# The start of a CIN tower kernel: shifted rows and pair tiles of the first chunk made by TensorE, stores and gathers moved

## The reference, cut to what matters

```python
e = jnp.stack([tbl_0[ids[:, 0]], ..., tbl_38[ids[:, 38]]], axis=1)      # (2048, 39, 16)
x0 = xk = e
for idx, (W, b) in enumerate([(w0, b0), (w1, b1), (w2, b2)]):           # W: (39, 39 or 64, 128)
    z = jnp.einsum('bhd,bkd,hks->bsd', x0, xk, W) + b[None, :, None]
    z = jax.nn.relu(z)
    if idx != 2:
        xk = z[:, :64, :]
        direct.append(z[:, 64:, :])
    else:
        direct.append(z)
z = jnp.sum(jnp.concatenate(direct, axis=1), axis=-1)                   # (2048, 256)
h = jnp.concatenate([z, dense_ctx], axis=1)
h = relu(h @ W_top1 + b_top1); h = relu(h @ W_top2 + b_top2); y = h @ W_top3
```

## Time and profile before

| | us |
|---|---|
| median of 3 runs | 2480.24 (2478.45 to 2482.26) |
| the profiled execution's own time | 2467.41 |
| its span, first to last instruction | 2465.7 |
| TensorE's mean granted clock in it, share of full | 0.997 |
| VectorE busy | 2229.2 (90%) |
| GpSimd busy | 1706.1 (69%) |
| ACT busy | 1484.1 (60%) |
| DMA, mean | 195 GB/s |

### The profile page before, as it was taken

How to read it: one execution, slowest core, us unless ns; L and a number is a source line. 1 busy time by engine, 2 the same in 40 slices (tenths; PEclk the granted TensorE clock), 3 DMA queues, 4 the chain that set the end, 5 groups by cost and what they waited for, 6 DMA issues and landing times.

```text
span 2465.7 us, 26690 instructions
## 1 busy us (share of the span) xinstructions
PE 2366.6 (96%) x7712; PEld 1456.0 (59%) x7712; DVE 2229.2 (90%) x1358; ACT 1484.1 (60%) x1766; POOL 1706.1 (69%) x1091
## 2 busy tenths in 40 slices
PE   0599999999999999999999999999999999999999
PEld 0266666666666666666666666666666666666653
DVE  0599999999999999999999999999999999999960
ACT  0366666666666666666666666666666666666642
POOL 6577777777777777777777777777777777754340
PEclk9999999999999999999999999999999999999999
DMA  2987878788787878878787887778778787877620
GB/s 70 249 229 183 211 211 211 188 216 224 189 204 213 217 183 213 221 199 196 214 223 188 207 217 211 187 210 224 195 199 220 214 185 209 218 205 186 201 63 0
DMA packets 380953, 481.10 MB, mean 195 GB/s; under 512 B 140683, under 2 KB 155771, under 8 KB 380853
## 3 DMA queue, kind: packets, MB, share of 16 engines
q1 hardware_dynamic: 260006, 275.13, 43.6%
q10 hardware_dynamic: 100480, 200.29, 28.8%
q0 software_dynamic: 20448, 5.45, 1.9%
HBM read 470.96 MB, written 9.84 MB: 195 GB/s over the span
## 4 chain that ended last, share of the span: by engine, by line
PE 95%; POOL 2%; DMA 2%; issue 1%; ACT 0%; DVE 0%; SPq 0%; ACTq 0%; POOLq 0%; DVEq 0%
PE z L735 46%; PE z L756 46%; POOL emb L394 1%; PE z L850 1%; PE xk L850 1%; DMA x_pairs<-x_transposed 1%; PE direct L850 1%; DMA x_diag<-x_transposed 0%; POOL lo_parts L244 0%; DVE prod L464 0%; DMA x_transposed<-emb 0%; ACT x_pairs L723 0%; DMA emb<-in_tbl,idx 0%; ACT hi_parts L586 0%; DMA idx<-in_ids 0%
## 5 line engine op out<-in xcount | busy, mean ns | idle before, releaser
L464 DVE TENSOR_TENSOR prod<-x_pairs,xk 128x2048 f32<-128x2048 f32 x640 | 1438.4, 2281 | 88.5 <-PE z L756 47.4
L735 PE MATMUL z<-prod,w_plain 128*128 128x512 f32 (+2 forms) x2688 | 1264.7, 595 | 91.6 <-DVE prod L464 91.6
L244 POOL TENSOR_TENSOR lo_parts<-prod,hi_parts 128x1024 fp32r<-128x1024 f32 x384 | 917.6, 2390 | 484.0 <-ACT hi_parts L586 458.3
L586 ACT CAST hi_parts<-prod 128x1024 fp32r<-128x1024 f32 x766 | 797.7, 1049 | 699.6 <-DVE prod L464 508.0
L756 PE MATMUL z<-hi_parts,w_lo 128*128 128x512 f32 (+1 forms) x1536 | 862.3, 561 | 1.1 <-DVE lo_parts L244 0.7
L394 POOL DMA_INDIRECT emb<-in_tbl,idx x624 | 698.9, 1120 | 192.5 <-issue 176.8
L735 PEld LDWEIGHTS z<-prod,w_plain 128*128 128x128 f32 (+2 forms) x2688 | 510.2, 190 | 491.1 <-issue 420.2
L756 PE MATMUL z<-hi_parts,w_hi 128*128 128x512 f32 (+1 forms) x1536 | 611.1, 398 | 0.0
L756 PE MATMUL z<-lo_parts,w_hi 128*128 128x512 f32 (+1 forms) x1536 | 606.5, 395 | 0.0
L756 PEld LDWEIGHTS z<-hi_parts,w_lo 128*128 128x128 f32 (+1 forms) x1536 | 289.9, 189 | 199.9 <-issue 151.0
L756 PEld LDWEIGHTS z<-lo_parts,w_hi 128*128 128x128 f32 (+1 forms) x1536 | 292.1, 190 | 193.0 <-issue 152.0
(11 more groups left out here) (64 smaller groups left out, 546.2 us busy)
## 6 DMA issues: line engine op xcount, KB each, us to landing
x_pairs<-x_transposed SPq DMA_DIRECT2D x64, 2432.0 KB, 16.5
x_pairs<-x_transposed ACTq DMA_DIRECT2D x64, 2432.0 KB, 18.9
x_diag<-x_transposed SPq DMA_DIRECT2D x128, 546.0 KB
x_diag<-x_transposed ACTq DMA_DIRECT2D x64, 546.0 KB
x_pairs<-x_transposed SPq DMA_DIRECT2D x64, 256.0 KB, 19.7
emb<-in_tbl,idx POOLq DMA_INDIRECT x624
x_diag<-x_transposed SPq DMA_DIRECT2D x128, 78.0 KB
x_transposed<-emb SPq DMA_DIRECT2D x16, 312.0 KB, 6.2
```

Source lines behind the costliest of these rows:

```text
L244: engine.tensor_tensor(lo_parts[0:rows, place:place + m, :], held[0:rows, at:at + m, :], hi, ALU.subtract).then_inc(done, 1)
L464: nc.vector.tensor_tensor(prod[0:rows, pos % RING, 0:n, :], a, xk.unsqueeze(1).broadcast_to([rows, n, N]), ALU.mult).then_inc(prod_ready, 1)
L586: nc.scalar.copy(hi_parts[0:rows, place:place + m, :], held[:, at:at + m, :]).then_inc(hi_ready, 1)
L735: return nc.tensor.matmul(z[n][:], w, held[0:rows, i, :], start=first, stop=last)
```

## The change

Chunk 0 of group 0 no longer gets its shifted rows, nor eight of its 20 pair tiles, from DRAM. When the first 39 gathers have landed, TensorE transposes the 32 examples' rows (16 transposes into `z[1]`), VectorE copies them to `rows0`, and TensorE multiplies selection matrices (made by VectorE from a banded identity that GpSimd makes first) with `rows0`: 7 shifted tiles, `xk0`, and pair tiles 12 to 19. ACT copies each from PSUM. SP stores the chunk's 32 rows first (`first_stored`), ACT the other 96 rows of the group (`xt_stored`); SP loads pair tiles 0 to 11 after `first_stored`.

Outside the first chunk: `load_chunk` loses its `store` argument. `store_group(bt)` now stands at the head of `load_chunk(bt, 0)`, so SP issues it at `c == 3` of its own loop, after the pair loads of `load_chunk(bt - 1, 3)`, with the wait for `xt_stored` right behind it. GpSimd gathers 14 fields ahead instead of 20; group 0 then takes 11, 11, 3 and 13 fields in its four chunks and starts group 2's at `c == 3` (`turn=3`); group 1 takes 13, 13, 10 and 10; from group 2 on the spread is as before, with the start at `c == 2`. VectorE's group 0 and GpSimd's groups 0 and 1 stand ahead of their loops.

```diff
-GATHERS_AHEAD = 20
+GATHERS_AHEAD = 14
+GATHERS_FIRST = [range(14, 25), range(25, 36), range(36, F), range(0, 13)]
+GATHERS_SECOND = [range(13, 26), range(26, F), range(0, 10), range(10, 20)]
 GATHERS_AT = [range(20, 30), range(30, F), range(0, 10), range(10, 20)]
+SPREAD_PAIRS = (16, 17, 18, 19, 12, 13, 14, 15)
+COPIED_PAIRS = 12
+SPREAD_EARLY = 3
...
+        spread_banks = [z[1], hi_copy[:, 0, :], hi_copy[:, 1, :]]
+        spread_to = ([x0_diag[0:R0, t, :] for t in range(T0)]
+                     + [x0_pairs[0][:, t, :] for t in SPREAD_PAIRS])
...
+            def first_chunk():
+
+                sp.wait_ge(gathered, 16 * F)
+                store_rows(sp, 0, 0, slice(0, CB), first_stored)
+                sp.wait_ge(first_stored, 16 * ST_DMAS)
+                sp.wait_ge(w_split, 3)
+                for half in range(2):
...
+                    sp.dma_start(x0_pairs[0][half * HALF:(half + 1) * HALF, 0:COPIED_PAIRS, :],
+                                 src.partition_broadcast(HALF)).then_inc(first_pairs_in, 16)
+                sp.wait_ge(xt_stored, 16 * ST_DMAS)
+
+            def load_chunk(bt, c):
...
                 if c == 0:
+                    store_group(bt)
                     sp.wait_ge(xt_stored, 16 * ST_DMAS * (bt + 1))
-                if not (isinstance(bt, int) and bt == c == 0):
-
-                    sp.wait_ge(summed2, sums)
+                sp.wait_ge(summed2, sums)
                 chunk = xt[:, bass.ds(first, N)]
                 for i in range(DIAG - 1):
                     diag_band(sp, chunk, i)
-                if store:
-                    store_group(bt + 1)
...
+                sp.wait_ge(prod_ready, slots)
                 pairs_half(sp, chunk, c, 0)
...
                     if c < CHUNKS - 1:
-                        load_chunk(bt, c + 1, c == 2 and not last)
+                        load_chunk(bt, c + 1)
                     elif not last:
                         load_chunk(bt + 1, 0)
...
-            def group(bt, fields_at):
+            def group(bt, fields_at, turn=2):
...
-                    if c == 2 and len(fields_at[c]):
+                    if c == turn and len(fields_at[c]):
                         start_group(bt + 2, False)
...
+            pool.wait_ge(first_stored, 16 * ST_DMAS)
+            pool.wait_ge(rows0_turned, 1)
             start_group(1, False)
             gather(range(0, GATHERS_AHEAD))
-            with pool.Fori(0, GROUPS - 2) as bt:
+            group(0, GATHERS_FIRST, 3)
+            group(1, GATHERS_SECOND)
+            with pool.Fori(2, GROUPS - 2) as bt:
                 group(bt, GATHERS_AT)
...
+            dve.wait_ge(rows0_turned, 1)
+            nc.vector.tensor_copy(rows0[:], z[1][0:F]).then_inc(rows0_ready, 1)
             dve.wait_ge(xk0_ready, 1)
-            late, split = products(0, x0_diag, xk0, 0, 0, [], 0, 0)
+            late, split = products(0, x0_diag, xk0, 0, 0, [], 0, 0, {0: QUAD, 1: T0})
...
+            act.wait_ge(gathered, 16 * F)
+            store_rows(nc.scalar, 0, 0, slice(CB, P), xt_stored)
+            take_spread(range(T0))
...
+            take_spread(range(T0, T0 + SPREAD_EARLY))
             hand_on(0, xk1, b0_sb, SL0)
             direct_0()
+            take_spread(range(T0 + SPREAD_EARLY, len(spread_to)))
+            act.wait_ge(spread_ready, len(spread_to))
+            act.wait_ge(xt_stored, 16 * ST_DMAS)
             load_last_band(0, 1)
...
+            for d in range(D):
+
+                ins = nc.tensor.transpose(z[1][0:F, d:N:D], emb[0:CB, d:F * D:D], ident[0:CB, 0:CB])
+            ins.then_inc(rows0_turned, 1)
+            pe.wait_ge(chosen_ready, T0 + 3)
+            pe.wait_ge(rows0_ready, 1)
+            spread_rows(range(QUAD))
+            nc.tensor.matmul(xk0[0:R0], by_diag[:, T0, :], rows0[:], start=True, stop=True
+                             ).then_inc(xk0_ready, 1)
+            spread_rows(range(QUAD, T0 + SPREAD_EARLY))
             pe.wait_ge(w0_summed, 2)
             pe.wait_ge(w_split, 3)
             pe.wait_ge(weights_in, 16 * WEIGHT_DMAS)
             layer0(0, 0, {V: 0, G: 0})
+            spread_rows(range(T0 + SPREAD_EARLY, len(spread_to)))
+            pe.wait_ge(spread_ready, len(spread_to))
```

More of the change, by code:

```diff
@@ L153, in build @@
         emb = sb("emb", [P, F * D])
+        ident = sb("ident", [F, F + WRAP])
+        rows0 = sb("rows0", [F, N])
+        by_diag = sb("by_diag", [F, T0 + 1, R0])
+        by_pair = sb("by_pair", [F, F + 1 - 2 * COPIED_PAIRS, HALF])
         w_plain = [sb(f"w{n}_plain", [P, len(PLAIN_TILES[n]), S]) for n in SPLITS]
@@ L245, in low_part, with chosen, store_rows @@
                                      hi, ALU.subtract).then_inc(done, 1)
+        spread_banks = [z[1], hi_copy[:, 0, :], hi_copy[:, 1, :]]
+        spread_to = ([x0_diag[0:R0, t, :] for t in range(T0)]
+                     + [x0_pairs[0][:, t, :] for t in SPREAD_PAIRS])
+        def chosen(first, *dims):
+            rows = ident[0:F, first:]
+            return bass.AP(tensor=rows.tensor, offset=rows.offset, ap=[rows.ap[0], *dims])
+        pair_columns = by_pair[:].rearrange("f g h -> f (g h)")
+        spread_by = ([by_diag[:, t, :] for t in range(T0)]
+                     + [pair_columns[:, (t - COPIED_PAIRS) * P:(t + 1 - COPIED_PAIRS) * P]
+                        for t in SPREAD_PAIRS])
+        def store_rows(engine, bt, first, parts, done):
+            cols = xt[:, bass.ds(first, P * D)].rearrange("f (b d) -> b f d", d=D)
+            rows = emb[:].rearrange("p (f d) -> p f d", d=D)
+            engine.dma_start(cols[parts, 0:F, :], rows[parts]).then_inc(done, 16)
+            engine.dma_start(cols[parts, F:F + WRAP, :], rows[parts, 0:WRAP, :]).then_inc(done, 16)
         def diag_band(engine, chunk, i):
@@ L288, in store_group @@
                 sp.wait_ge(gathered, 16 * F * (bt + 1))
[L289 to L294, removed]
+                store_rows(sp, bt, first, slice(0, P), xt_stored)
+            def first_chunk():
[4 more added lines that the diff above has]
+                for half in range(2):
+                    src = xt[half:half + 2 * COPIED_PAIRS, 0:N].rearrange(
+                        "(t two) n -> t two n", two=2)[:, 0, :]
+                    sp.dma_start(x0_pairs[0][half * HALF:(half + 1) * HALF, 0:COPIED_PAIRS, :],
+                                 src.partition_broadcast(HALF)).then_inc(first_pairs_in, 16)
+                sp.wait_ge(xt_stored, 16 * ST_DMAS)
+            def load_chunk(bt, c):
                 first = ahead(bt * (P * D) + c * N)
@@ L347, in load_top @@
                     sp.dma_start(dst, src).then_inc(top_weights_in, 16)
[L349 to L352, removed]
+            first_chunk()
             def group(bt, last):
@@ L379, in _ @@
         def _(pool):
+            nc.gpsimd.memset(ident[:], 0.0).then_inc(ident_zero, 1)
+            for i in range(2):
+                pool.wait_ge(ident_zero, i + 1)
+                nc.gpsimd.affine_select(out=ident[:], in_=ident[:], compare_op=ALU.not_equal,
+                                        fill=1.0, base=i * F, pattern=[[-1, F + WRAP]],
+                                        channel_multiplier=1
+                                        ).then_inc((ident_zero, ident_ready)[i], 1)
             def load_indices(bt):
@@ L488, in splits_of, with products @@
                 return here
-            def products(n, copies, xk, slot, pos, late, split, chunk):
+            def products(n, copies, xk, slot, pos, late, split, chunk, spread_in={}):
                 first_tile, rows, tiles = (FIRST_TILE, P, TX) if n else (L0_FIRST, R0, T0)
                 for k, first in enumerate(first_tile):
+                    if k in spread_in:
+                        dve.wait_ge(spread_ready, spread_in[k])
                     product(slot + k, pos + k, copies[0:rows, first:min(first + QUAD, tiles), :],
@@ L530, in group @@
                     copies = x0_pairs[c % 2]
-                    dve.wait_ge(x0_pairs_in[c % 2],
-                                16 * X0_PAIRS_DMAS * (bt * (CHUNKS // 2) + c // 2 + 1))
+                    first = isinstance(bt, int) and bt == c == 0
+                    if first:
+                        dve.wait_ge(first_pairs_in, 32)
+                        dve.sem_inc(x0_pairs_in[0], 16 * X0_PAIRS_DMAS)
+                    else:
+                        dve.wait_ge(x0_pairs_in[c % 2],
+                                    16 * X0_PAIRS_DMAS * (bt * (CHUNKS // 2) + c // 2 + 1))
                     dve.wait_ge(xk_ready[0], chunk + 1)
-                    late, split = products(1, copies, xk1, slot, pos, [], split, chunk)
+                    spread_in = {FIRST_TILE.index(t): T0 + QUAD * (i + 1)
+                                 for i, t in enumerate(SPREAD_PAIRS[::QUAD])} if first else {}
+                    late, split = products(1, copies, xk1, slot, pos, [], split, chunk, spread_in)
                     slot, pos = slot + SLX, pos + SLX
@@ L552, in group @@
```

(25 more changed lines are left out.)

27 lines of the change are left out of this document (21 added, 6 removed).

## The result

The changed kernel takes 2668.11 us (2667.10 to 2670.39), the kernel before 2480.68 in the same comparison: ratio 1.0758, 95% interval 1.0739 to 1.0776, slower by 187 us. The profiled execution of the changed kernel took 2667.10 us, its span is 2665.4, 199.7 longer than that of before.

A forecast was written before the change was run, and what follows sets the result against it. TensorE, busy 96% of the span, was taken as the bound. 173 (13 stands) + 0.7 + 2.5 + 6.2 - 17.8 = +164.6 us on the profiled 2467.41 gives 2632; carrying 12.8 to the median gives 2645 us, bounds 2610 to 2700.

The forecast's parts named there:

- The sign and the cause: Slower, chance 0.92: at `c == 2` GpSimd's gathers wait for the store behind the pair loads, 13 times, 173 us.
- The price of one stand: TensorE idle for late gathers at `c == 2`: 11.5 us standing plus 1.8 for the clock, 13.3 us [11.3 to 16.7].
- Why the store is late: SP's queue: the store, issued at about 741.4, is queued behind 2.7 MB of pair loads and lands at 765.5.
- ACT's wait: ACT waits for the store before the last band: 2.5 us in group 0, 0.7 in group 14, elsewhere inside the stall.
- Thirteen gathers: Chunks with thirteen gathers, in groups 0 and 1: 2.05 us each, three times, 6.2 us [4 to 12].
- The start: Ahead of TensorE's first full chunk: 17.8 us saved [12 to 21].
- five matmuls of 0.9 us: Start, after the copy to `rows0` at 58.0: four tiles and `xk0` done at 62.5, first product at 62.8.
- has worked since 54: Start: TensorE's six plain matmuls taken at full clock, so 11.0 us from the first product to `xk1`, at 73.8.
- The transposes: Start: 16 transposes on TensorE at the lower clock, 0.22 us each, 3.5 us [2.5 to 6.2], to 57.4.
- the first layer-1 product: Start: VectorE begins it at 74.5 [74 to 79.5] instead of 93.7, 19.2 us less.
- the stand's clock term: After each stand TensorE begins at the lower clock, four matmuls in 3.58 us instead of 1.72 to 1.8: 1.8 us.
- The signs named before: 13 TensorE dips, 13 GpSimd waits of some 15 us, store landing about 24, group period 156.5, half clock, first layer-1 product 74.5.

The follow-up runs named there:

- a_store_back: Changed kernel with the next group's store back between band loads and pair loads at `c == 2` from group 1 on; 2461.52 us, ratio 0.9969.
- b_store_moved: Kernel before with only the store moved to the head of `load_chunk(bt, 0)`, behind the pair loads; 2670.02 us, ratio 1.0813.
- c_store_ahead: As a_store_back, but the store issued after the wait for the chunk's first product, directly ahead of the pair loads; 2575.61 us, ratio 1.0433.
- i_one_queue: c_store_ahead with ACT's half of chunk 3's pair loads also issued by SP, behind the store; 2536.04 us, ratio 1.0274.
- d_turn3: Changed kernel with every group gathering 13, 13, 0 and 13 fields and starting the next but one group at `c == 3`; 2566.19 us.
- e_start_only: a_store_back with the store at its old place in every group, 20 gathers ahead and the old spread; 2449.43 us, ratio 0.9918.
- f_alloc_only: Kernel before with only the change's four new buffers allocated, unused; 2453.85 us, ratio 0.9938.
- j2_warm: e_start_only plus nine unused fp32 matmuls on TensorE ahead of the transposes, released behind GpSimd's 31st gather; 2453.64 us, ratio 0.9935.
- k2_padded: e_start_only with `rows0` and the selection matrices extended from 39 to 128 partitions, zeros in the added rows; 2440.58 us, ratio 0.9882.

## Why the prediction was right, step by step

- **The sign and the cause**: GpSimd's wait for the store at `c == 2` in 13 groups, named before. a_store_back and b_store_moved show it from both sides.
- **The price of one stand**: 13.3 forecast, 11.5 of standing and 1.8 for the clock. TensorE's 13 stands last 9.8 to 13.2 us, 12.1 on average; in the chunk shown the store landed 26.6 us after the pair loads' issue, where I had 25.6. The clock cost more than 1.8: behind a stand TensorE works at half for 3.0 to 6.1 us, 4.6 on average (5.7 in the chunk shown, 3.3 in the earlier trace rows), which costs 2.3. That makes 14.4. In b_store_moved, where nothing else differs, the whole is 200.7 us for 14 stands and group 14's 2.5: 14.2 each, of which 12.0 are standing and 2.1 the clock.
- **Why the store is late**: half right. I priced only what is ahead in SP's queue. c_store_ahead and i_one_queue split it: 18.0 us with ACT's pair loads beside it and nothing ahead, 7.1 with neither, 22.8 with both.
- **ACT's wait**: 2.5 forecast in group 0, 5.6 in the trace; 0.7 in group 14, where the trace has a chunk 2.6 us longer; in the other groups some 1 us by d_turn3, hidden in the stand.
- **Thirteen gathers**: 2.05 forecast, 1.9 to 3.1 measured in d_turn3; the three such chunks of the changed kernel cost 1.7, 2.9 and 3.2, 7.8 in all, where I had 6.2.
- **The start**: 17.8 forecast, 4.4 measured (e_start_only against f_alloc_only). This is the term that was mis-sized most. The step that failed is "five matmuls of 0.9 us": I read "x4" in the earlier trace rows as four matmuls, but an fp32 matmul stands as two in these rows. And I put TensorE at the full clock since it "has worked since 54"; it stayed at half through 19 us of 39-row matmuls. The stretches of this trace read 1.00 there, because its record of the clock begins with the first rise, at 80.0; the pace tells it: four rows ("x4") take 3.62 us, as they do in j2_warm at a recorded 0.50. What this cost is shown by k2_padded: 8.9 us less with the clock up from 62 us on. The changed kernel's rows:

```profile
56.85 2.02 PE L885 MATMUL z<-rows,by_diag 39*117 39x512 f32 x2 [0.87 <-DVE rows L581]
58.67 3.62 PE L885 MATMUL hi_copy<-rows,by_diag 39*117 39x512 f32 x4
...
65.74 2.29 DVE L513 TENSOR_TENSOR prod<-x_diag,xk 117x2048 f32<-117x2048 f32 x1 [9.04 <-PE xk L897]
...
84.87 4.48 DVE L513 TENSOR_TENSOR prod<-x_pairs,xk 128x2048 f32<-128x2048 f32 x2 [8.78 <-ACT xk L678]
...
92.15 1.04 ACT L657 CAST hi_parts<-prod 128x1024 fp32r<-128x1024 f32 x1 [2.16 <-issue]
```

  The first product is at 65.74, not 62.8, and `xk1`, not the pairs, comes last at 84.8. The transposes took 1.3 us where I had 3.5. Then ACT's last copies and DMA issues hold its first rounding back, 7.3 us behind the product instead of 3.25. So `xk1` was ready 11 us later than forecast, and the first layer-1 product, named as a sign at 74.5, started at 84.87. The misreading doesn't touch the stand's clock term, which compares equal rows.
- **What I had not**: the addresses, 15 us less; and 17 chunks of 36.1 instead of 35.56 us, with TensorE waiting 0.3 us for GpSimd in them, whose cause stays open.
- **The signs named before**: the 13 dips and GpSimd's 13 waits (15.2 to 17.4 us, some 15 forecast), the store's landing (22.8, about 24), the period of a group (157.9, 156.5) and the half clock in each stand are there. The first layer-1 product is not.
- **The total is nearer than its terms, and that is luck.** Between the two profiled executions the change costs 199.7 us; I had 164.6, 35 too few. Of these 35 the stands account for 14, the start for 13, group 0, group 14 and the thirteen gathers for 6 or 7; the addresses gave 15 back. What is left, some 16, are the 36.1 us chunks and losses near the stands that no run explains. In the comparison the loss is only 187.4, since the kernel before ran 12 us slower there; and the 12.8 us that I carried from its profiled execution to its median are not in the changed kernel, whose profiled execution lies 1.0 us under its median. Without them the forecast would have been 2632 against 2668.11.

## What to carry to other kernels

A DMA's place in the queue is part of the schedule: when a store moves, ask what is ahead of it in its own queue, what large load runs beside it on the other one, and who waits for its landing with work queued behind the wait. In a kernel whose busiest engine has no slack, a wait that recurs in each group weighs more than anything gained once at the start. Compare such kernels at the same buffer addresses, or measure the buffers alone.

## What the runs showed of the hardware

- TensorE's granted clock stayed at half (1.2 GHz) while matmuls over 39 rows kept it busy 4.00 of 4.00 us (j2_warm, recorded 0.50 from 57 to 80.5 us), and fell from full to half at 86.8 us in the middle of a run of them without a gap (the changed kernel). With zero rows added up to 128 the same matmuls went at half pace until 62 us and at full pace behind that (k2_padded). The Trainium skill ("TensorE: Matmul & The Clock Gate", Part 1: The HAM clock gate) ties the clock to how busy the engine has been; here, busy in the profile was not enough.
- An fp32 matmul of 512 columns stands as two rows in the time line: two rows for each of the 16 selection matmuls, 0.86 us each at half pace and 0.43 at full (the changed kernel, k2_padded).
- Small pieces beside 2 KB pieces of another queue: a store of 64-byte pieces takes 18.0 (c_store_ahead) instead of 7.1 us (i_one_queue).
- One queue alone moved 2 KB pieces at 213 GB/s (i_one_queue), two at 332 (the kernel before), with the engines shown as busy in both, 1.06 and 1.04.
- Where buffers lie in SBUF moves the pace of a matmul-bound chunk: 35.80 us in the kernel before, 35.56 in f_alloc_only for the same instructions.
